# A non-local block in split fp32: two products in matmuls of 256 columns in place of 512, and new SBUF places for the matmul operands

## The reference

```
q = einsum('bchw,dc->bdhw', x, theta_w) + theta_b        # 256 planes, 1024 positions
xpool = maxpool2(x)                                      # 256 positions
k = einsum('bchw,dc->bdhw', xpool, phi_w) + phi_b
v = einsum('bchw,dc->bdhw', xpool, g_w) + g_b
p = softmax(einsum('bdn,bdm->bnm', q, k) * 256 ** -0.5)  # 1024 x 256 per image
vp = einsum('bdm,bnm->bdn', v, p)
out = einsum('bdhw,cd->bchw', vp, z_w) + z_b + x
```

## Time and profile before

| | |
|---|---|
| median of 3 runs | 2090.24 us (2089.25 to 2090.63) |
| the profiled execution | 2089.69 us |
| its span, first to last instruction | 2087.9 us |
| TensorE busy | 2064.6 us, 13,976 matmuls |
| VectorE, ScalarE, GpSimd busy | 1560.8, 1291.6, 1375.8 us |
| mean granted TensorE clock | 0.997 of full |

### The profile page before, as it was taken

The page is one execution under the profiler, slowest core; times in us unless marked ns, Lnnn a source line. Parts: engine busy times, 40 slices in busy tenths (PEclk is TensorE's granted clock), DMA queues, the critical chain, the costliest instruction groups (busy, mean ns, idle before and its releaser), DMA issues.

```text
span 2087.9 us, 41365 instructions
## 1 busy us (share of the span) xinstructions
PE 2064.6 (99%) x13976; PEld 1909.7 (91%) x13976; DVE 1560.8 (75%) x2620; ACT 1291.6 (62%) x2228; POOL 1375.8 (66%) x833
## 2 busy tenths in 40 slices
PE   8899999999999999999999999999999999999997
PEld 7899999999999999999999999999999999999997
DVE  8787777787777877777877778777778777787765
ACT  6566566665665665666655656656666556566553
POOL 4676666676666766666766667766667666677653
PEclk9999999999999999999999999999999999999999
DMA  6556556656556555566465565555664655655535
GB/s 222 200 177 206 178 185 221 214 178 211 170 202 231 175 206 182 180 221 218 174 211 171 201 231 176 205 184 178 221 221 171 211 171 202 230 179 203 188 116 182
DMA packets 212904, 407.22 MB, mean 195 GB/s; under 512 B 12688, under 2 KB 15760, under 8 KB 212880
## 3 DMA queue, kind: packets, MB, share of 16 engines
q1 hardware_dynamic: 212736, 406.90, 56.8%
q10 hardware_dynamic: 144, 0.01, 0.0%
HBM read 272.64 MB, written 134.22 MB: 195 GB/s over the span
## 4 chain that ended last, share of the span: by engine, by line
PE 94%; DVE 2%; DMA 1%; POOL 1%; ACT 0%; issue 0%; SPq 0%; DVEq 0%; POOLq 0%
PE bank L836 94%; DVE pt_raw L653 1%; DMA x_bot<-x 0%; POOL x_split_lo L535 0%; DVE pooled L625 0%; DMA x_bot<-z_wt 0%; DMA x<-x 0%; DVE x_bot L671 0%; DVE x_top L671 0%; SPq L253 0%; ACT probs L442 0%; POOL att_lo L553 0%; DVE att_f L684 0%; DVE att_f L682 0%; DVE z_lo L694 0%
## 5 line engine op out<-in xcount | busy, mean ns | idle before, releaser
L535 POOL TENSOR_TENSOR x_split_lo<-x,x_split_hi 128x1024 fp32r<-128x1024 f32 x255 | 614.8, 2417 | 268.4 <-ACT x_split_hi L339 262.8
L836 PE MATMUL bank<-att_hi,z_hi 128*128 128x256 f32 x1792 | 505.0, 282 | 8.3 <-DVE x_bot L671 5.2
L836 PE MATMUL bank<-att_lo,z_hi 128*128 128x256 f32 x1792 | 503.9, 281 | 0.0
L836 PE MATMUL bank<-att_hi,z_lo 128*128 128x256 f32 x1792 | 503.9, 281 | 0.0
L653 DVE STREAM_TRANSPOSE pt_raw<-probs 32x256 f32<-32x256 f32 x1024 | 446.1, 436 | 20.7 <-ACT probs L442 4.1
L836 PE MATMUL bank<-x_split_hi,theta_hi 128*128 128x512 f32 x1024 | 398.5, 389 | 2.2 <-POOL x_split_lo L535 1.6
L836 PE MATMUL bank<-x_split_hi,theta_lo 128*128 128x512 f32 x1024 | 398.4, 389 | 0.0
L836 PE MATMUL bank<-x_split_lo,theta_hi 128*128 128x512 f32 x1024 | 398.4, 389 | 0.0
L671 DVE TENSOR_TENSOR x_top<-bank,x_top 128x512 f32<-128x512 f32 x512 | 335.6, 687 | 81.6 <-PE bank L836 73.6
L553 POOL TENSOR_TENSOR att_lo<-att_f,att_hi 128x512 fp32r<-128x512 f32 (+1 forms) x192 | 284.9, 1490 | 163.0 <-ACT att_hi L378 163.0
L339 ACT ACTIVATE x_split_hi<-x 128x1024 fp32r<-128x1024 f32 x256 | 270.5, 1057 | 151.3 <-PE bank L836 147.1
(11 more groups left out here) (71 smaller groups left out, 4081.7 us busy)
## 6 DMA issues: line engine op xcount, KB each, us to landing
x<-x SPq DMA_DIRECT2D x256, 512.0 KB, 3.8
x_top<-x SPq DMA_DIRECT2D x128, 512.0 KB, 6.9
x_bot<-x SPq DMA_DIRECT2D x128, 512.0 KB, 4.9
out<-x_top SPq DMA_DIRECT2D x128, 512.0 KB, 3.5
out<-x_bot SPq DMA_DIRECT2D x128, 512.0 KB, 6.5
x_top<-theta_wt SPq DMA_DIRECT2D x4, 256.0 KB, 5.1
x_top<-g_wt SPq DMA_DIRECT2D x4, 256.0 KB, 4.1
x_bot<-z_wt SPq DMA_DIRECT2D x4, 256.0 KB, 5.9
```

The source lines that it names most:

```text
L535: nc.gpsimd.tensor_tensor(flat(lo), flat(x_chunk(s, c)), raw(flat(hi)), ALU.subtract).then_inc(x_ready, 1)
L836: last = nc.tensor.matmul(dst, stationary(a), moving(b), start=start and n == 0, stop=stop and n == len(PRODUCTS) - 1, skip_group_check=re ...
```

## The change

q and attention are issued as two matmuls of 256 columns each in place of one of 512. In `project_q` the two halves of the columns follow each other within each of the channel blocks; in `attend` all matmuls of the first half of the columns come before those of the second. The signals to other engines stay behind the last matmul of the same group. The buffers are declared in another order:

| operand (moving, stationary) | place before (moving, stationary) | place now |
|---|---|---|
| q: x_split, theta | 0, 0 | 3, 0 |
| k: xp, phi | 3, 0 | 0, 1 |
| v: g, xp | 6, 3 | 3, 0 |
| scores: k, q | 3, 0 | 3, 0 |
| attention: pt, vt | 0, 0 | 3, 0 |
| output: att, z | 3, 0 | 3, 0 |

All buffers declared behind `phi` (the unsplit x chunks, `x_top`, `x_bot`, `pooled`, `probs`, `pt_raw`, `att_f`, `still`) move up by one line, and `still` is 192 columns wide in place of 224.

```diff
-STILL = 224
+STILL = 192
...
-        sb("pad_moving", [P, 16], f32)
-        xp = [sb(f"xp_{s}", [P, KT, M], f32r) for s in ("hi", "lo")]
+        sb("pad_a", [P, 16], f32)
+        att = [sb(f"att_{s}", [P, 7, HB], f32r) for s in ("hi", "lo")]
         k = [sb(f"k_{s}", [P, DT, M], f32r) for s in ("hi", "lo")]
-        att = [sb(f"att_{s}", [P, 7, HB], f32r) for s in ("hi", "lo")]
-
+        gw = [sb(f"g_{s}", [P, KT, D], f32r) for s in ("hi", "lo")]
+        xs = [[sb(f"x_split_{s}{i}", [P, KC, H], f32r) for s in ("hi", "lo")] for i in range(XS)]
+        pt = [sb(f"pt_{s}", [P, MT, H], f32r) for s in ("hi", "lo")]
...
-        gw = [sb(f"g_{s}", [P, KT, D], f32r) for s in ("hi", "lo")]
-
-        sb("pad_stationary", [P, 32], f32)
+        sb("pad_b", [P, 32], f32)
         theta = [sb(f"theta_{s}", [P, KT, D], f32r) for s in ("hi", "lo")]
+        zw = [sb(f"z_{s}", [P, 7, TB * P], f32r) for s in ("hi", "lo")]
+        vt = [sb(f"vt_{s}", [P, MT, D], f32r) for s in ("hi", "lo")]
+        q = [sb(f"q_{s}", [P, DT, H], f32r) for s in ("hi", "lo")]
+        xp = [sb(f"xp_{s}", [P, KT, M], f32r) for s in ("hi", "lo")]
+        sb("pad_c", [P, 16], f32)
         phi = [sb(f"phi_{s}", [P, KT, D], f32r) for s in ("hi", "lo")]
-        zw = [sb(f"z_{s}", [P, 7, TB * P], f32r) for s in ("hi", "lo")]
-        q = [sb(f"q_{s}", [P, DT, H], f32r) for s in ("hi", "lo")]
-        vt = [sb(f"vt_{s}", [P, MT, D], f32r) for s in ("hi", "lo")]
-        pt = [sb(f"pt_{s}", [P, MT, H], f32r) for s in ("hi", "lo")]
-        xs = [[sb(f"x_split_{s}{i}", [P, KC, H], f32r) for s in ("hi", "lo")] for i in range(XS)]
...
-                        last = product(q_banks(turn, s)[m][:, :], lambda a: theta[a][:, kt, m * P:(m + 1) * P],
-                                       lambda b: x_split(s, c)[b][:, i, :], kt == 0, kt == KT - 1)
+                        for h in range(2):
+                            last = product(q_banks(turn, s)[m][:, h * HB:(h + 1) * HB],
+                                           lambda a: theta[a][:, kt, m * P:(m + 1) * P],
+                                           lambda b: x_split(s, c)[b][:, i, h * HB:(h + 1) * HB], kt == 0 and h == 0, True, True)
...
-                    for mt in range(MT):
-                        last = product(a_bank[m][:, :], lambda a: vt[a][:, mt, m * P:(m + 1) * P],
-                                       lambda b: pt[b][:, mt, :], mt == 0, mt == MT - 1)
+                    for h in range(2):
+                        for mt in range(MT):
+                            last = product(a_bank[m][:, h * HB:(h + 1) * HB], lambda a: vt[a][:, mt, m * P:(m + 1) * P],
+                                           lambda b: pt[b][:, mt, h * HB:(h + 1) * HB], mt == 0, mt == MT - 1)
```

## The result

The changed kernel takes 2063.86 us (median of 4, 2061.04 to 2064.01) against 2090.43 before: a ratio of 0.9869, 95% interval 0.9857 to 0.9880. It is 26.6 us faster. The forecast was 2128 and slower; the time lies outside its range and on the other side.

A forecast was written before the change was run, and what follows sets the result against it. TensorE's dense row of matmuls was taken to bound the kernel for 94% of the time. Terms of +31.9, +5.9 and +0.3 us summed to +38.1, giving 2128 us against a median of 2090.24; range 2113 to 2140.

The forecast's parts named there:

- Step (1): q and attention: two halves at 117.7 ns cost 8.7 more than one of 512; +31.9 us, bounds -26.8 to +49.6.
- Step (4): Output product and scores keep places 3 and 0, only their buffers' distance changes, so their price stays; 0.
- Step (2): v's operands move from 6 and 3 to 3 and 0, its price from 113.75 to 117.7 ns; +5.9 us.
- Step (3): k's operands move from 3 and 0 to 0 and 1; no change taken, bounds -5.9 to +3.6 us.
- Step (5): Start and end outside the TensorE-bound stretch: some halves on the path, narrower fillers; +0.3 us.
- Step (6): Buffers behind phi move one line; other engines' slack covers any loss, TensorE's added instructions need no wait; 0.
- D: Rival: x_split at place 3 frees its stream from the weight load, halves near 109.7 ns; 2070 us, chance 0.10.
- C: Rival: halves of q and attention run at v's price, +2.9 us, v still +5.9; 2099 us, chance 0.06.
- A: The forecast's own case: terms as summed, with a few us for k; 2128 us, chance 0.60.
- rival B: Places are worth nothing, v stays at 113.75 ns, 2122 us; or k falls to it too, 2116; chance 0.16.

The follow-up runs named there:

- e7: The changed kernel with its moving operands at place 5 in place of 3; 2091.8 us.
- e11: e4 with one filler matmul more ahead of the first q chunk of each half; 2100.0 us.
- e6: The kernel before with output, scores and v at places 6 and 3, q and attention still 512 columns at 0 and 0; 2096.9 us.
- e10: The changed kernel with attention alone back in matmuls of 512 columns at places 0 and 0; 2125.1 us.
- e4: The changed kernel with xp at place 3, g at 6, phi at 0 (every product at 3 and 0 but v at 6 and 3), fillers of 224 columns; 2122.98 us.
- e2: The kernel before with only the width changed: q and attention in halves of 256 columns, buffers in the old order; 2109.7 us.
- e12: e5 with fillers of 192 columns in place of 224; 2084.9 to 2088.4 us, one of 10 executions at 2113.9.
- e8: The changed kernel with its moving operands at place 4 in place of 3; 2165.3 us.
- e13: The changed kernel with fillers of 160 columns in place of 192; 2063.5 us, ratio 0.9866 to the kernel before.
- e1: The changed kernel's buffers with q and attention back in matmuls of 512 columns; 2083.7 to 2088.3 or 2114.9 to 2116.5 us.
- e5: e4 with q and attention in matmuls of 512 columns; 2085.0 to 2088.4 us (7 of 10) or 2112.7 to 2113.1.
- e9: The changed kernel mirrored, all products at places 6 and 3 except k at 3 and 0; 2062.8 us, ratio 0.9868 to the kernel before.

## Why the prediction was wrong

**What bounds the kernel** was right: TensorE in one dense row, and the time is its prices from start to start. The rebuilt image of 63.73 us was right too, but it only showed that the prices add up, not what they depend on.

**Step (1), q and attention in halves, failed: +31.9 us forecast, 0 measured.** "I take the output product's price, because it agrees in width, type and both places." Agreement in these does not fix a price: the same pair of places costs 113.3 or 117.8 by what ran before (shown within the traces of the changed kernel, e7 and e11). The 0 lies a little below the bound from v's row (227.5 a pair, +2.9 us) and well above the one from the fillers (-26.8).

**Step (4), output and scores at 0, is where the gain lay: -28 us.** They were held to be untouched since their places were. What the change took away was their neighbour, groups of 512 columns with both operands at an even place, behind which they enter at 117.8 and stay (the kernel before and e6, where the turn itself is in the trace; in e10 one such product among six costs the whole 61 us). Taking it away was needed but is not enough: e4 has no such group either and stays at 117.8. What the changed kernel has besides is the passage from k at 0 and 1 to attention, in which the price falls, and a v at its neighbours' places, behind which it is not lost.

**Step (2), v: +5.9 forecast, -0.6 measured** (48 x 0.4 ns an image). That the places 3 and 0 cost more than 6 and 3 was taken from a right row as a rule: it is so in the kernel before, which stands in B; in A it is the reverse (e2, e12). **Step (3), k: 0**, measured 0, by luck: at 0 and 1 k is slow in A, where it would have been fast at 3 and 0. xp is k's moving and v's stationary operand, and in no run here are k and v both at the fast price; this costs 48 x 4.4 ns = 0.2 us an image in the changed kernel, in v or in k. **Step (5)** (+0.3) was small as said: the start is 0.4 us shorter and the end 1.4 longer. **Step (6)** held: TensorE has no idle time in the middle image.

**The rivals.** D had the right side and nearly the time (2070), but by a mechanism that did not happen: a pair had to cost less than 225.0 and costs 226.7. C had the halves' price right and kept output at 117.7. A's sum was not idle arithmetic: e4, where the rhythm stays B and v keeps 6 and 3, took 2122.98, and 2122 is what rival B gave for that case. What was missing was a rival in which the price of a row in the table belongs to the row before it. A sign stood in the trace: 24 scores and v follow each other, and v's mean of 113.75 over 48, above its later 113.3, means that its first matmuls had still been slow. I read this mean as a constant.

The prediction read the two read ports of the Trainium skill (page "SBUF — State Buffer", "Who interferes with whom") as places being worth nothing. That reading is not what the runs show: 120.0 at 4 and 0 against 113.3 at 3 and 0 (e8, changed). The gap rule of the Trainium skill for single matmuls ("TensorE: Matmul & The Clock Gate", "Back-to-back issue gap") gives 109.2 and 215.8 ns; the lowest steady prices in any run here are 113.3 and 226.7.

**What stays open.** What the rhythm is physically was not settled; a relation in time between the weight loads and the moving stream is a guess. Nor is it known how many such conditions there are (e6, e10), why the passage through k turns it from B to A and not back in the changed kernel and e13, and both ways in e7, nor why the executions of e1, e5 and e12 part at the start. That e9 and the changed kernel differ in nothing was measured to about 0.1%.

## What to carry to other kernels

When TensorE is the bound, take the price of a matmul from start to start, look whether one product has the same price everywhere in the trace, and ask what ran before it. A price read from a dense row belongs to the sequence it was read in; before adding up hundreds of matmuls at it, look for a stretch of the same product behind other neighbours or behind an idle gap. For narrow fp32r products, do not put both operands at even 64-byte lines (120.0 in e8); but odd beside even promises nothing by itself, since e4 has it everywhere and is slower than the kernel before. Try narrow products without wide ones at even places beside them, keep neighbouring products at the same two places, and time a small delay: in e11 it was worth more than the work it added.

## What the runs showed of the hardware that was not expected

- fp32r matmuls of 256 columns behind a weight load each showed three steady prices at the full clock: 113.3 ns, 117.8 ns, and 120.0 when both operands start at an even 64-byte line (e8; q in e2). Of 512 columns: 226.7 with both even, 232.8 at 3 and 0 (e1, e5).
- Which of 113.3 and 117.8 holds depends on the places and on what ran before, and can last for thousands of matmuls. 3 and 0 was fast with 6 and 3 slow (e2, e12) or with 0 and 1 slow (changed), and slow with the other fast (before, e1); but both were also slow together (e6, e10, the changed kernel from 95 to 157 us). The price turned across an idle gap (1.18 us in the changed kernel), behind one bf16 filler (e11), in passing from one product to another (e4, e7), and behind wide matmuls with both operands at even lines (e6).
- One kernel can have two times 1.3% apart, drawn in each execution (e5: 2085 to 2088 and 2113); the granted clock of its ten executions was 0.996 to 0.998, with 0.997 and 0.998 in the upper group.
